# Selective scan and ternary FFN on one core: banks per channel half, softplus summed on TensorE, FFN input by tiles

## The reference, cut to what matters

```python
x = x + ssm(ctx, z=layernorm(x))           # x: (4, 256, 256), ctx: (4, 256, 128)
x = x + ffn(layernorm(x))

# ssm: 256 channels e, 16 states n, 256 steps l, 4 batches
u     = silu(causal_conv4(in_proj_w @ ctx) + conv_b)
dt, B, C = split(x_proj_w @ u)             # 8, 16, 16 rows
delta = softplus(dt_proj_w @ dt + dt_proj_b)
state[n] = state[n] * exp(-delta * exp(A_log)[n]) + delta * u * B[n]     # along l
y     = (sum_n state[n] * C[n] + D * u) * silu(z)

# ffn: 256 -> 1024 -> 256, each linear layer "bit_linear"
gate, val = silu(bit_linear(x, gate_w, gate_b)), bit_linear(x, val_w, val_b)
out = bit_linear(gate * val, out_w, out_b)
# bit_linear: each row of x is scaled by 127 / max|row| and rounded, w is rounded to
# -1, 0, 1 times mean|w|, then the product and both scales back
```

## Time and profile before

| | |
|---|---|
| timed runs | 219.12, 219.13, 220.28 us |
| the profiled execution | 218.7 us, span of the instructions 216.8 |
| mean granted PE clock | 0.795 of full |
| DVE busy | 176.1 us |
| POOL, PE, ACT busy | 137.5, 149.0, 133.4 us |
| start to first scan | 0 to 25.6 us |
| scans 0 to 63 | 25.6 to 177.6 us |
| last scan to the end | 177.6 to 216.8 us |

### The profile page before, as it was taken

One profiled execution on the slowest core, in us unless ns is written; L12 is line 12 of the kernel. 1 busy time (PEld: TensorE's weight loads), 2 busy tenths in 40 slices (PEclk: granted clock), 3 DMA queues, 4 the chain that ended last, 5 costly groups with the idle time before them and its releaser, 6 DMA issues.

```text
span 216.8 us, 2402 instructions
## 1 busy us (share of the span) xinstructions
PE 149.0 (69%) x706; PEld 92.4 (43%) x706; DVE 176.1 (81%) x269; ACT 133.4 (62%) x207; POOL 137.5 (63%) x134
## 2 busy tenths in 40 slices
PE   6983049871793687776107987737886478899983
PEld 5531035351451575566105444425463165335452
DVE  3787999959939969999999397996489998757771
ACT  2569656896189869761307579365975206286672
POOL 5039499997965994967849999993069004690000
PEclk9995558996555579696755587966699969999999
DMA  4994953450331110040024031322000000000002
GB/s 117 243 336 135 331 177 82 146 206 29 142 98 48 33 63 0 12 136 2 0 91 151 3 87 78 126 89 80 0 5 26 0 0 0 4 23 15 9 24 73
DMA packets 12689, 17.44 MB, mean 80 GB/s; under 512 B 3468, under 2 KB 9012, under 8 KB 12678
## 3 DMA queue, kind: packets, MB, share of 16 engines
q1 hardware_dynamic: 12678, 17.30, 24.9%
HBM read 16.11 MB, written 1.19 MB: 80 GB/s over the span
## 4 chain that ended last, share of the span: by engine, by line
DVE 22%; PE 21%; issue 8%; ACT 4%; POOL 2%; DVEq 0%; POOLq 0%
DVE state L934 4%; PE work L1275 4%; PE ysum L1189 4%; DVE wstate L944 3%; DVE gam L1015 2%; DVE xhat L849 2%; PE decay L1099 2%; DVE pool_state L934 2%; PE work L1099 2%; PE work L1282 2%; DVE wstage L1010 2%; PE work L1315 2%; PE decay L1275 1%; ACT gT L748 1%; PE cwide L1210 1%
## 5 line engine op out<-in xcount | busy, mean ns | idle before, releaser
L497 POOL TENSOR_TENSOR drive<-du,b_wide 128x1024 f32<-128x1024 f32 x31 | 73.8, 2395 | 3.1 <-DVE du L925 2.8
L679 ACT ACTIVATE decay<-delta,aneg 128x510 f32<-128x510 f32 x64 | 43.0, 685 | 29.5 <-DVE state L934 15.0
L934 DVE TENSOR_TENSOR_SCAN state<-decay,drive 128x512 f32<-128x512 f32 x44 | 52.4, 1208 | 2.7 <-ACT decay L679 2.4
L1189 PE MATMUL ysum<-ident,wstate 128*128 128x128 f32 x176 | 34.3, 343 | 9.8 <-DVE wstate L944 9.8
L1189 PEld LDWEIGHTS ysum<-ident,wstate 128*128 128x128 f32 x176 | 27.9, 180 | 18.0 <-DVE wstate L944 13.0
L944 DVE TENSOR_TENSOR wstate<-state,cwide 128x512 f32<-128x512 f32 x44 | 29.0, 662 | 7.5 <-issue 7.5
L507 POOL TENSOR_TENSOR pool_wstate<-pool_state,c_wide 128x1024 f32<-128x1024 f32 x10 | 23.6, 2361 | 13.7 <-PE ysum L1189 11.6
L1210 PE MATMUL cwide<-cparts,sel 128*128 128x512 bf16 x22 | 10.5, 476 | 26.0 <-DVE wstate L944 14.2
L934 DVE TENSOR_TENSOR_SCAN pool_state<-decay,drive 128x512 f32<-128x512 f32 x20 | 24.3, 1216 | 2.2 <-ACT decay L679 2.2
L1275 PE MATMUL work<-ternary,qT 128*128 128x512 bf16 x46 | 15.1, 416 | 3.8 <-ACT wstage L729 1.6
L1099 PE MATMUL work<-ident,wstage 128*128 128x128 f32 x80 | 12.5, 301 | 5.4 <-ACT ternary L703 2.8
(11 more groups left out here) (186 smaller groups left out, 290.5 us busy)
## 6 DMA issues: line engine op xcount, KB each, us to landing
b_wide<-bc_rows SPq DMA_DIRECT2D x16, 512.0 KB, 4.3
c_wide<-bc_rows SPq DMA_DIRECT2D x10, 256.0 KB, 3.4
x_in<-in_x SPq DMA_DIRECT2D x2, 512.0 KB, 4.0
wstage<-in_L_ffn_gate_w SPq DMA_DIRECT2D x1, 1024.0 KB, 7.6
wstage<-in_L_ffn_val_w SPq DMA_DIRECT2D x1, 1024.0 KB, 10.1
wstage<-in_L_ffn_out_w SPq DMA_DIRECT2D x1, 1024.0 KB, 8.9
ctx_in<-in_ctx SPq DMA_DIRECT2D x2, 256.0 KB, 3.7
out<-wtap SPq DMA_DIRECT2D x4, 128.0 KB, 1.7
```

The source lines that it names most:

```text
L497: nc.gpsimd.tensor_tensor(drive[:, m % NDR], du[:, m // NS], rows.unsqueeze(1).to_broadcast([P, EH, W]), ALU.mult).then_inc(s_drive, 1)
L679: nc.scalar.activation(v[:, :, 1:L], d[:, :, 1:L], ACT.Exp, scale=aneg[:, eh, n:n + 1]).then_inc(s_decay, 1)
L934: nc.vector.tensor_tensor_scan(dst, decay[i % ND][:], drive[:, i // EH % NDR, i % EH], 0.0, ALU.mult, ALU.add).then_inc(s_scan, 1)
L1189: last = nc.tensor.matmul(ysum[:, k, eh * P:(eh + 1) * P], lhsT=src[:, k * P:(k + 1) * P], rhs=ident[:], start=start and k % LB == 0, stop ...
```

## The change

It has these parts:
- `ysum` becomes one bank per channel half, all four tiles in each; the turned sums go to `ysum[:, eh, k]`.
- Group 1's softplus: POOL's four operations go. ACT makes 1 + mag and its negative (`softplus_rest`), PE sums four terms in a work bank with the identity (`softplus_sum`), DVE multiplies the bank with u by halves (`delta_u`, steps 23 and 27), ACT copies delta out (`delta_out`, steps 25 and 28). Decay 32 and 33 wait for that copy.
- Rounding of the three weights goes by halves; many constants change; `work_tiles` derives its order from them.
- Group 0's normalisation goes from DVE to ACT (`normalise_x1`, step 36); `rstd(1)` makes a shift for it; input is at DVE step 35, clips at 32, 37, 40.
- `scales` takes two operations instead of three. `ffn_scale_parts` makes fewer, broadcast operations and frees the dequantising scales last.
- The tail: group 1's gate and add for channel half 0 (`late_gates`, waits for sum 62 alone), then half 1 tile by tile with its variance (`late_input`); rstd, input, turns and token parts by single tiles (parts of tiles 2 and 3 together); group 0's last turn and output ahead of them; warming products 2 and 3.
- The last tile: a peak per half, the second half quantised and copied by DVE, and the output product starts on the first half.

```diff
-PE_PROJ, ACT_U, ACT_PROJ, ACT_SPLIT = 10, 9, 14, (18, 20)
-PE_PRE, ACT_PRE = (15, 16), (17, 19)
-POOL_SOFTPLUS = (11, 12, 13, 14)
-DVE_SPLIT, DVE_DELTA = (13, 17), 27
-ACT_WSUM, PE_WSUM, DVE_WSUM = (0, 2, 6), 12, 15
-ACT_ROUND = (21, 23, 27)
-DVE_CLIP = (32, 34, 39)
-DVE_GATED, DVE_STATS, DVE_INPUT = 33, 35, 37
-PE_COLS, ACT_COLS = 38, 41
-PE_GATE, ACT_GATE = (39, 44, 51, 53), (44, 47, 56, 58)
-PE_VAL, DVE_VAL, DVE_VAL2 = (45, 48, 59, 60), (46, 48, 60, 62), (47, 49, 61, 62)
-ACT_QUANT, PE_TURN, ACT_TURN = (52, 54, 65, 68), (49, 54, 65), (53, 61, 67)
-PE_OUT, DVE_OUT = (50, 58, 67), (51, 60)
-TURNS, WARM = (6, 6), (20, 3)
+PE_PROJ = 11
+ACT_U = 10
+ACT_SPLIT = (18, 27)
+PE_PRE = (14, 18)
+ACT_MAG = (20, 21)
+ACT_LOG = (20, 24)
+ACT_REST = (20, 24)
+PE_SUMD = (21, 24)
+ACT_DELTA = (25, 28)
+DVE_SPLIT = (14, 22)
+DVE_DELTA = (23, 27)
+PE_WSUM = 8
+DVE_WSUM = 9
+ACT_ROUND = (18, 21, 23, 25, 27, 28)
+DVE_CLIP = (32, 37, 40)
+DVE_INPUT = 35
+ACT_NORM = 36
+ACT_RND = 40
+PE_COLS = 36
+PE_GATE = (38, 39, 43, 44, 51, 51, 53, 53)
+PE_VAL = (45, 45, 48, 48, 58, 58, 60, 60)
+DVE_VAL2 = (47, 51, 61, 62)
+ACT_QUANT = (48, 53, 65, 68)
+PE_TURN = (50, 57, 65)
+DVE_OUT = (52, 60)
+WARM = (2, 3, 0, 0)
...
-        ysum = pb("ysum", [P, GT, DI])
+        ysum = pb("ysum", [P, EH, GT, P])
...
+            def softplus_rest(eh):
+                act.wait_ge(s_expln, 2 * (EH + eh) + 1)
+                link(nc.scalar.activation(du[:, 1, eh], mag[:, eh], ACT.Copy, bias=1.0))
+                nc.scalar.activation(du[:, 1, eh], du[:, 1, eh], ACT.Copy, bias=1.0, scale=-1.0).then_inc(s_wneg, 1)
+            def delta_out(eh):
+                t = wait_full(act, f"dl{eh}")
+                act.wait_ge(s_du, EH + eh + 1)
+                release(nc.scalar.activation(delta[:, 1, eh], t[:], ACT.Copy), f"dl{eh}")
...
+            def normalise_x1():
+                act.wait_ge(s_rstd, 2)
+                for t in range(GT):
+                    nc.scalar.activation(hn[:, t], x1[:, t], ACT.Identity, bias=shift[:, 1, t:t + 1],
+                                         scale=nv[:, 1, t:t + 1]).then_inc(s_hn, 1)
...
+            def delta_u(eh):
+                t = wait_full(dve, f"dl{eh}")
+                nc.vector.tensor_tensor(du[:, 1, eh], t[:], u[:, 1, eh], ALU.mult).then_inc(s_du, 1)
...
+            def softplus_sum(eh):
+                name = f"dl{eh}"
+                t = work_tile(name)
+                pe.wait_ge(s_wneg, eh + 1)
+                for j, src in enumerate((mag[:, eh], du[:, 1, eh], lnw[:, eh], pre[:, eh])):
+                    last = nc.tensor.matmul(t[:], lhsT=ident[:], rhs=src, start=j == 0, stop=j == 3)
+                fill(last, name)
...
             weigh(2 * UNITS - 1)
-            gate_and_add(1)
-            for h in range(BG):
-                dve.wait_ge(s_half[h], 1)
-                variance(x1, h * LB, (h + 1) * LB)
-            for h in range(BG):
-                ffn_input(1, h * LB, (h + 1) * LB, 2 + h)
+            late_gates(0, 0, GT)
+            late_input(0)
             ffn_output(0, GT - 2)
-            for t in range(GT):
+            late_input(1)
+            ffn_input(1, 0, 1, 2)
+            late_input(2)
+            ffn_input(1, 1, 2, 3)
+            late_input(3)
+            ffn_output(0, GT - 1)
+            ffn_input(1, 2, 3, 4)
+            for t in range(GT - 1):
                 for c in range(CH):
                     ffn_value(1, t, c)
+                if t == 0:
+                    ffn_input(1, 3, 4, 5)
                 ffn_scale(1, t)
...
+            last_scale()
+            ffn_output(1, GT - 3)
+            ffn_output(1, GT - 2)
+            last_hidden()
+            ffn_output(1, GT - 1)
...
             wait_weighed(pe, G * UNITS - 1)
             warm(WARM[0])
+            ffn_turn(0, GT - 1)
+            warm(WARM[1])
+            ffn_output(0, GT - 1)
+            warm(WARM[2])
             ffn_half(1, 0)
-            warm(WARM[1])
+            warm(WARM[3])
...
                     for c in range(CH):
                         ffn_activations(1, 0, c, "gate")
-                    ffn_scales(1, 0)
                     for c in range(CH):
                         ffn_activations(1, 0, c, "val")
+                    ffn_half(1, 1)
+                    ffn_scales(1, 0)
                     wait_read(pe, "acol10")
```

More of the change, by code:

```diff
@@ L104, in work_tiles @@
     first = ["inp", "ctx0", "conv0", "xin", "xproj", "dtw", "xc00", "conv1", "proj0", "pre00", "pre01", "ctx1"]
-    scans = ["xc10", "xc11", "proj1", "wsum", "pre10", "pre11", "z0", "z1"]
-    scans += [f"w{m}{k}" for m in "gvo" for k in range(4)]
     def tile(g, t, *kinds):
@@ L111, in tile @@
         return sum((names[kind] for kind in kinds), [])
-    scans += ["q00", "q01", "acol00"] + tile(0, 0, "gate") + tile(0, 1, "gate")
-    scans += tile(0, 0, "val") + tile(0, 1, "val") + tile(0, 0, "turn", "out") + ["z2", "z3"]
-    scans += tile(0, 2, "gate") + tile(0, 3, "gate") + tile(0, 1, "turn", "out")
-    scans += tile(0, 2, "val") + tile(0, 3, "val") + tile(0, 2, "turn", "out")
-    last = ["q10"]
+    scans = []
+    for i in range(PE_OUT[-1] + 1):
+        if i % TAPS == 0 and i < EH * TAPS:
+            scans += [f"xc1{i // TAPS}"]
+        scans += [f"z{k}" for k in range(BG) if PE_Z[k] == i]
+        scans += ["proj1"] * (i == PE_PROJ) + ["wsum"] * (i == PE_WSUM)
+        scans += [f"pre1{eh}" for eh in range(EH) if PE_PRE[eh] == i]
+        scans += [f"dl{eh}" for eh in range(EH) if PE_SUMD[eh] == i]
+        scans += [f"w{'gvo'[k // 4]}{k % 4}" for k in range(12) if PE_ROWS[k] == i]
+        scans += ["q00", "q01", "acol00"] * (i == PE_COLS)
+        for t in range(GT - 1):
+            scans += tile(0, t, "turn") if PE_TURN[t] == i else []
+        for t in range(GT - 1):
+            scans += tile(0, t, "out") if PE_OUT[t] == i else []
+        scans += ["z2", "z3"] * (i == PE_ZLATE)
+        scans += [f"gate0{k // CH}{k % CH}" for k in range(CH * GT) if PE_GATE[k] == i]
+        scans += [f"val0{k // CH}{k % CH}" for k in range(CH * GT) if PE_VAL[k] == i]
+    last = tile(0, GT - 1, "turn", "out") + ["q10"]
     for t in range(GT):
         last += tile(1, t, "gate")
-        if t == 0:
-            last += ["acol10"]
         if t > 1:
@@ L124, in work_tiles @@
         last += tile(1, t, "val")
+        if t == 0:
+            last += ["q11"]
         if t > 1:
@@ L127, in work_tiles @@
         if t == 0:
-            last += tile(0, GT - 1, "turn")
+            last += ["acol10", "acol11"]
         if t == 1:
-            last += ["q11", "acol11"] + tile(0, GT - 1, "out")
+            last += ["q12", "q13", "acol12"]
     for t in range(GT - 2, GT):
@@ L224, in block_program @@
         gam = sb("gam", [P, 8, GT])
+        peak = sb("peak", [P, 2])
         tscale = sb("tscale", [P, 2, GT])
@@ L438, in rstd @@
             def rstd(k):
-                t0, t1 = ((0, B * LB), (0, GT), (0, LB), (LB, GT))[k]
+                t0, t1 = ((0, B * LB), (0, GT), *((t, t + 1) for t in range(GT)))[k]
                 pool.wait_ge(s_var, k + 1)
@@ L579, in _ @@
             ffn_scale_parts(1, 0)
+            rstd(4)
             ffn_scale_parts(1, 1)
+            rstd(5)
+            ffn_scale_parts(1, 2)
             residual(1)
@@ L758, in _ @@
             projections(0)
-            softplus_parts(0, 0)
-            softplus_parts(0, 1)
+            for eh in range(EH):
+                magnitude(0, eh)
+                softplus_logs(0, eh)
             link(nc.scalar.activation(aneg[:], alog[:], ACT.Exp))
@@ L1247, in ffn_half @@
                 t = work_tile(name)
-                pe.wait_ge(s_q, GT * g + 2 * h + 2)
+                n = 1 if g else 2
+                pe.wait_ge(s_q, GT * g + n * h + n)
                 for d in range(2):
-                    for k in range(2):
-                        o = (d * 2 + k) * P
-                        last = turn(t[:, o:o + P], hn[:, 2 * h + k, d * P:(d + 1) * P])
+                    for k in range(n):
+                        o = (d * n + k) * P
+                        last = turn(t[:, o:o + P], hn[:, n * h + k, d * P:(d + 1) * P])
                 fill(last, name)
```

330 lines of the change are left out of this document (184 added, 146 removed).

## The result

| | before | changed kernel |
|---|---|---|
| timed runs, median | 219.7 us (219.12 to 220.4) | **212.44 us** (207.69 to 216.63) |
| ratio, 95% interval | | **0.952** (0.939 to 0.965) |
| the profiled execution, its span | 218.7, 216.8 | 210.57, 208.8 |
| granted PE clock, mean | 0.795 | 0.842 |

Faster by 4.8% by the ratio, by 3.3% by the medians. The prediction said 210.8 (207.0 to 215.6), and 210.6 for the profiled execution. The four runs of the changed kernel lie 9 us apart, and their order is that of the granted clock: 207.69 at 0.849, 210.57 at 0.842, 214.32 at 0.823, 216.63 at 0.809. (Ratios leave out runs more than 1.5% above the fastest of their kernel, here two of the four; medians do not.) The same kernel timed again, six runs beside those of its experiments, gave **212.86** (211.4 to 215.8), ratio 0.968 (0.962 to 0.973).

A forecast was written before the change was run, and what follows sets the result against it. DVE bounds the scans to 178 us, then a chain of small steps, TensorE, and a closing chain. 3.5 - 0.5 + 1.0 + 2.5 + 0.7 + 0.9 = 8.1 off 218.7 gives 210.6; stated 210.8, range 207.0 to 215.6.

The forecast's parts named there:

- the wait of 3.6 for the spread of C: Sign: DVE's wait for TensorE's spread of C, 3.64 before, would still be there, partly filled by clip 1 (1.36).
- TensorE's granted clock after the scans: Sign: the prediction would be wrong if this clock was 0.5 once the scans end.
- part 1: Group 1's softplus moved off GpSimd, to the end of scan 27: 3.5 us earlier.
- decay 29: New DVE wait of 2.2 at scan 29 behind ScalarE's queue, against 1.7 of work gone: 0.5 later.
- part 2: Turn to group 0's FFN, normalisation moved to ScalarE: 1.3 gained, less 0.3; 1.0 in the sum.
- part 3: Steps 40 to 63: output 0's wait of 2.04 goes, other wait 0.3 longer, smaller scales 0.8: 2.5 gained.
- Rival A: Softplus sums on TensorE stay at 1.2 GHz, second ends 4.3 later: 215.1 us; chance 0.15.
- Part 4: The tail after scan 63: 0.7 gained up to group 1's products and 0.9 at the end, 1.6 together.
- rival C: TensorE's tail counts in full if parts are not late, 4.8 instead of 1.6: 207.6 us; chance 0.10.
- the 0.7 of this term: Tail, group 1's FFN products: those of tile 1 start at 14.5 after scan 63 against 15.2, 0.7 gained.
- Rival B: TensorE falls to 1.2 GHz at group 1's first products, tail's 1.6 becomes a loss of 2: 214.4; chance 0.12.
- D: Slower: TensorE's queue stops at four holds on unread banks, delaying the spread of C: up to 223.4; chance 0.08.

The follow-up runs named there:

- pool_softplus: Changed kernel with group 1's softplus on GpSimd and DVE again, and the steps of the kernel before for that part: 217.48 us.
- dve_norm: Changed kernel with group 0's normalisation on DVE again (step 37) and clip 1 at step 34: 211.01 us.
- old_places: Changed kernel with quantising, turns and output 0 of group 0 (steps 49 to 54) at their steps of before: 216.12 us.
- warm_20: Changed kernel with 20 warming products instead of 2 at the head of the tail: 215.46 us, ratio 0.978.
- fill_tail: Changed kernel with eleven more unread products in TensorE's idle pieces ahead of group 1's bias products: 208.82 us, ratio 0.949.
- again: Changed kernel timed and profiled once more, nothing edited: 212.86 us, ratio 0.968.
- round_26: Changed kernel with the last half of a weight rounding on ScalarE at step 26 instead of 28: 211.35 us.
- whole_last: Changed kernel with group 1's last FFN tile in one piece, quantised and copied on ScalarE alone: 213.53 us.

## Why the prediction was right

The time was forecast to 0.8% and the profiled execution to 0.1 us, but partly by luck, since large errors cancel: the middle gained 4 us more than forecast, the tail and the start took it back. Two of the prediction's own signs went against it. Scan 63 ended at 169.9, near the 171 forecast, and no table load stands at Identity; but the wait of 3.6 for the spread of C was to stay and went, and TensorE's granted clock after the scans, which was not to be 0.5, was 0.5 for a stretch of the tail in eight of nine profiles. Step by step:

| step | forecast | measured | by |
|---|---|---|---|
| part 1, to scan 27 | 3.5 | 4.4 | both profiles; 4.6 by `pool_softplus` without its early wait |
| decay 29 and part 2, to scan 42 | 0.5 | 1.8 | both profiles |
| part 3, 42 to 63 | 2.5 | 4.4, 4.6 | both profiles; the move alone 1.3 |
| tail | 1.6 | 0.3, -3.6 | first, second profile |
| ahead of scan 1 | 0 | -2.7, 0.1 | first, second profile |

*Part 1.* The waits came as worked out queue by queue: 1.30 for 1.3, 1.08 for 1.2, 2.19 for 2.2, the split's gone, both sums within 5 us. Rival A (cold sums) did not come: the half clock lasted for one product of the first sum. The wait of 0.6 at scan 21 and the 0.5 for the second sum did not come, which more than covers the 0.9 above the forecast. Taken out alone, the part costs 0.9 more from scan 27 to 42: 1.9 of work and 1.4 of the first clip (2.08 again, see below) come back, the 2.2 for decay 29 go.

*Part 2.* The idle time of 4.33 was forecast as 4.7, and Identity loads no table: ScalarE has nine table loads before and after. The page "ScalarE: Activation LUTs" of the Trainium skill (Table sets), which has identity in every set, agrees with that. What failed is the sign of the step: I gave the normalisation's move 1.0, and `dve_norm` shows that the kernel is 0.8 to 1.3 better without it. The price of the wait for the spread of C was carried over from the old order, in which it was 3.64; in the new one it is 0.93. The 1.8 of this stretch, row by row: 3.6 of wait and 1.9 of work for delta went, 2.2 came in for decay 29, the scales take 0.9 more, the three clips together 0.4 more (the first 1.4 less, the last 1.9 more), and small ones 0.3. The prediction's sum had none of these changes of length. The shorter first clip belongs to part 1, since `pool_softplus` has its 2.08 back. And one reading was wrong: beside the two normalisations of 0.73 in the tail GpSimd was not idle, it worked on two columns for the power of rstd (0.71 from 184.56).

*Part 3.* The wait for output 0 went as said, but it was worth 1.3 (`old_places`). The wait of 3.81 at the spread fell to 2.87 and 2.62 where I had it grow by 0.3; it is 2.23 even with the old places (32.4 for 35.0, before). Products by single halves in PE's queue may be the cause; no run isolates it, so this 1.2 to 1.5 against the forecast stays open. The smaller scales brought 1.3, a third of a microsecond a tile, where I had 0.8.

*Part 4.* The first product of group 1 starts 11.0 after scan 63's start against 12.3, 0.5 less than forecast: group 0's output 2 was full later, since PE ran the last sums and the turn at half clock (1.97 and 1.73 for eight, 1.25 and 1.04 before). That lead is gone by tile 1, as rival C's argument against it said, and more than I had it: its products start 16.6 after scan 63's start against 16.2, so the 0.7 of this term is -0.4. The end, from DVE's first value product of the last tile, is 9.6 to 9.8 long against 10.3 (206.51 to 216.8): 0.5 to 0.7 for a forecast of 0.9. What failed in it are the halves: without them it is 9.3 to 9.4. Both value banks are full within a microsecond, and I had let the scale come sooner although the first peak stands between them. The rest, the output product that begins on the first half and the shorter scales, is worth 0.9.

*Rival B* had the mechanism and the price right, and the place wrong. It put the fall at group 1's first products, for lack of 20 warming products, cost 3.6. It lies some 7 us later. `warm_20` has the products and the fall, `fill_tail` the fall no more. I gave it 0.12, and it was the usual case: of the nine profiles with an unfilled tail (`warm_20` among them) only the first escaped, and in `again`, `round_26` and `whole_last` it cost 3.4 to 3.9 against that one or `fill_tail`, in `pool_softplus` and `dve_norm` 2.5, in `old_places` 6.5. From none to 6.5, it could make most of the 9 us between the changed kernel's four runs; the runs without a profile don't show it. My ground against it was a row in which PE was busy for 0.34 of 2 us and kept its clock; ahead of this fall it had been busy for 5.33 of 8 us, in pieces, and as much in the profile that escaped. "TensorE: Matmul & The Clock Gate" in the Trainium skill (Part 1: activity releases the throttle, idleness brings it back) speaks for the mechanism, and its remark that the same kernel differs from run to run fits the one profile that escaped; the runs here add that in `again` it fell with no idle piece longer than 0.62 us in the 8 us ahead of it.

*Rivals C and D.* The tail did not count in full, and nothing got slower by PE's queue: of the four holds I had listed only the one behind delta 1 shows (2.19).

*Not counted as part of the change*: the 2.7 us ahead of scan 1 in the first profile. `again` has 30.8 there, before 30.9; but two of the thirteen profiles of the changed kernel and its edits start late and there is one profile of before, so that the kernel before never does this is not shown.

## What to carry to other kernels

A schedule change that thins out TensorE's work can cost its clock afterwards, in the place where it is needed most; look at what the engine does ahead of its densest stretch, and fill idle pieces there with products nobody reads, where they lie (eleven were worth 4 us; twenty in another place cost 2.6). When runs of one kernel lie 4% apart, put two profiles side by side before any theory of the change: the medians of most single edits said little here beside the profile's stretches. A stretch has its own spread too (here up to 1.5 us from scan 1 to 27), so name the wait in it that differs before the edit gets the credit. A wait's price belongs to the queue order in which it was read: once the order changes, the edit that was to hide it may be the one to take back.
